# A gated relational graph convolution on one core: the root product moved behind the last relation, three sweeps of edge sums in place of five

## Chip, cores and metric

One core of one Trainium2 chip. The metric is device time of one execution in microseconds (us), median over runs; lower is better. Engines: PE (TensorE), DVE (VectorE), ACT (ScalarE), POOL (GpSimd) and SP (SyncE, which only issues DMAs here).

## What is computed

x is 1250 x 1024, there are 20000 edges (src, dst, type 0 to 7), sorted by dst, and ten 1024 x 1024 matrices: eight relation weights, root, and w_gate (2048 x 1024, two more).

```python
h = maximum(layernorm(x), 0)
u = h @ root + bias
for r in range(8):
    mask = (edge_type == r)
    sums = segment_sum(h[src] * mask[:, None], dst, 1250)
    cnt  = segment_sum(mask, dst, 1250)
    u = u + (sums / maximum(cnt, 1)[:, None]) @ weight[r]
z = concatenate([u, h], 1) @ w_gate + b_gate
out = x + tanh(u) * z + h * (1 - z)
```

## The kernel before

All matrices go through PE as pairs of float16 numbers (a high and a low part), three matmuls for each product of a 128-row block. The relation is applied before the sum: y = h @ weight[r] is written to DRAM (`y_rows`), and the edges then gather rows of y.

**The order of the work** is a list of 325 units, written out by tables of unit numbers. A unit is one piece of a product: all engines walk the same loop `for n in range(NU)`, and each does there what the tables put at n. `GEMMS` is the order of the ten products, `FIRST` the unit at which each starts. The first three (`PLAIN = 3`) and the last are plain products, 20 units of 24 matmuls each. The seven between are Winograd block products (quarters of the matrices, seven phases), 35 units of 12 matmuls each. Before the change:

- plain: rel0 in units 0 to 19, rel1 20 to 39, root 40 to 59
- block products: rel2 from 60, rel3 from 95, rel4 from 130, rel5 from 165, rel6 from 200, rel7 from 235, gate_h (the half of w_gate that meets h) from 270
- plain: gate_u (the half that meets u) in units 305 to 324

PE writes unit n into PSUM bank n % 4 and waits until unit n - 4 has been taken out (`FREED`). In block products DVE does the adding (`finish`, L1069), and for the relations ACT and DVE split the result in high and low part (L766, L1024). Weights are landed, measured (`peek`, L683), split (ACT L716, DVE L937) and, for block products, added in quarters (DVE L953) beside the products.

**The sums.** Edges are cut into 80 groups: ten tiles of 125 destinations by eight relations. A sweep is a set of relations that are summed for all ten destination tiles in turn; `SWEEPS` lists them, and a sweep can start only when its last relation is in DRAM. In a start phase DVE turns dst and type into a key and a row number for each edge (`edge_keys`, L884 to L908; the loop over sweeps at L897 to L906 shifts both for each later sweep), and POOL scatters the edges into a table. Each group is padded to tiles of 128 edges. For each tile POOL copies an index (L623), gathers rows of y (L633) into a ring of five buffers `G`, and makes a one-hot matrix (L641, at the end of a sweep L669). PE multiplies: four matmuls of 512 columns (L1278) into banks 4 and 5 and one for the count (L1281). `AGG_AT[g]` is the unit after which PE does the first tile of group g, `REST_AT[g]` that of its other tiles. DVE then divides and adds to u in `add_group` (L1145 to L1147), at unit `REST_AT[g]`. The first tile of the next group waits for this, since the banks are the same.

**u** (1250 x 1024, float32) lies in DRAM, `u_rows`. A step is one destination tile in one sweep: SP loads the tile to one of three buffers `ub` (`load_u`, L412), the sweep's groups are added, SP stores it (`store_u`, L421). In sweep 0 the load fetches what the root product wrote. After the last sweep u is closed tile by tile: DVE `row_scale` (L1154 to L1159), ACT `u_high` (L774), DVE `u_low` (L1163), ACT `tanh_u` (L780, in place, then stored), PE `turn_u` (16 transposes in two halves, L1313, both into bank 7), ACT and DVE `u_out` (L787, L1172) into hT, from where gate_u reads. `SPLIT_U` and `TURN_U` give the units of these; they are at least three units apart per tile, and `TURN_U` of the last tile is unit 306, inside gate_u. There is one buffer `uhl` for the split u.

**SP's queue** is in order too: at each n it does its landings, then u's stores and loads, then waits for the unit's result (`store`, L398 for y, L402 for the z rows and, before, root's). A wait in it holds back all that follows.

## Time and profile before

| | us |
|---|---|
| median of 3 runs | 1406.08 |
| lowest, highest | 1405.66, 1414.51 |
| span of the profiled execution | 1407.7 |
| PE busy in it | 1291.5 (92%) |
| DVE, POOL, ACT busy | 952.5, 754.8, 409.0 |
| mean granted clock of PE | 0.974 of full speed |
| moved by DMA | 269.44 MB |

The span runs from the first to the last instruction of one profiled execution, and is 1.6 us over the median of the unprofiled runs. Busy time of PE holds matmuls at the lower clock too; DMA issues and waits are not busy time.

### The profile page before, as it was taken

The numbers are of one execution on the slowest core, as the hardware profiler recorded it, in microseconds if no ns is written. First come the engines' busy times: TensorE is split into PE (matmuls) and PEld (weight loads), VectorE is DVE, ScalarE is ACT, GpSimd is POOL, SyncE is SP. The second block draws the span as 40 slices with busy tenths as digits, with TensorE's granted clock in tenths as the row PEclk, the third lists the DMA queues.
The fourth block names the chain that finished last, engine by engine and source line by source line (L and its number), as shares of the span: only waits on it lengthen the run. The fifth ranks groups of instructions, "written<-read, shape, count | busy, mean of one in ns | idle before, by whom it ended". The sixth has DMA issues, their size and how long they took to land.

```text
span 1407.7 us, 20144 instructions
## 1 busy us (share of the span) xinstructions
PE 1291.5 (92%) x6205; PEld 651.6 (46%) x6205; DVE 952.5 (68%) x1260; ACT 409.0 (29%) x501; POOL 754.8 (54%) x837
## 2 busy tenths in 40 slices
PE   2978899999999999999998999998999989786898
PEld 1434344444444445555554445454445445343565
DVE  6889678366565667775675577646666778765777
ACT  5344123214132422321332043223222323432000
POOL 2423088786878426686687558664756464320000
PEclk9998899999999999999999999999999999998999
DMA  6442125215224348777875887769889977648872
GB/s 220 154 173 101 44 52 156 69 45 171 54 59 122 114 158 277 238 237 247 277 209 161 292 267 246 238 210 305 279 254 303 312 230 240 204 138 248 239 226 90
DMA packets 112355, 269.44 MB, mean 191 GB/s; under 512 B 22558, under 2 KB 23061, under 8 KB 112268
## 3 DMA queue, kind: packets, MB, share of 16 engines
q1 hardware_dynamic: 78284, 185.88, 40.2%
q0 software_dynamic: 33984, 82.40, 20.4%
q8 instruction: 55, 0.90, 0.3%
q14 instruction: 32, 0.26, 0.1%
HBM read 203.66 MB, written 87.30 MB: 207 GB/s over the span
## 4 chain that ended last, share of the span: by engine, by line
PE 61%; DVE 13%; DMA 10%; issue 7%; POOL 4%; ACT 2%; DVEq 1%; SPq 1%; POOLq 1%; ACTq 0%
PE ps L1320 52%; PE ps L1278 8%; DMA early<-y_rows,pair 7%; DVE W L937 2%; DMA early<-u_rows 1%; POOL onehot L641 1%; DVE hT L990 1%; DMA W<-in_L_gnn_weight_dram 1%; POOL early L633 1%; DVE hT L985 1%; PE ps L1313 1%; POOL pair L623 1%; DVE early L1147 1%; DVE early L1069 1%; DVE early L1163 1%
## 5 line engine op out<-in xcount | busy, mean ns | idle before, releaser
L1320 PE MATMUL ps<-W,hT 128*128 128x512 f16 (+2 forms) x4740 | 1076.0, 385 | 13.0 <-DVE W L937 13.0
L1320 PEld LDWEIGHTS ps<-W,hT 128*128 128x128 f16 (+2 forms) x4740 | 479.9, 104 | 537.8 <-issue 43.4
L633 POOL DMA_INDIRECT early<-y_rows,pair x200 | 242.1, 1211 | 194.5 <-PE ps L1281 152.4
L606 POOL DMA_INDIRECT table_rows<-edges,table_i x160 | 240.5, 1503 | 100.6 <-issue 100.6
L1278 PE MATMUL ps<-early,onehot 128*125 x800 | 205.9, 385 | 26.6 <-POOL onehot L641 13.1
L641 POOL TENSOR_SCALAR onehot<-iota_d,pair 128x125 f16<-128x125 f16 x185 | 159.9, 864 | 64.2 <-DMA early<-y_rows,pair 58.2
L766 ACT ACTIVATE yhl<-early 128x512 f16<-128x512 f32 x120 | 75.3, 628 | 355.3 <-DVE early L1069 194.2
L937 DVE SCALAR_TENSOR_TENSOR W<-W,wsc 128x2048 f16<-128x2048 f32 x62 | 146.5, 2364 | 13.8 <-ACT W L716 13.7
L1278 PEld LDWEIGHTS ps<-early,onehot 128*125 x800 | 106.8, 137 | 100.4 <-issue 46.6
L716 ACT ACTIVATE W<-W,wsc 128x2048 f16<-128x2048 f32 x62 | 122.6, 1990 | 50.9 <-DVE wsc L932 20.3
L683 ACT ACTIVATE peek_out<-W 128x1024 bf16<-128x1024 f32 x80 | 84.2, 1052 | 94.7 <-DMA W<-in_L_gnn_weight_dram 72.7
L1147 DVE SCALAR_TENSOR_TENSOR early<-ps,inv,early 125x1024 f32<-125x1024 f32 x80 | 102.7, 1284 | 2.8
L1024 DVE TENSOR_TENSOR yhl<-early,yhl 128x512 f16<-128x512 f32 x120 | 83.6, 696 | 0.7 <-ACT yhl L766 0.5
L1069 DVE SCALAR_TENSOR_TENSOR early<-ps,Q 128x512 f32<-128x512 f32 x60 | 41.4, 689 | 50.4 <-PE ps L1320 42.5
L581 POOL TENSOR_TENSOR early<-early 128x1024 f16<-128x1024 f32 (+1 forms) x10 | 27.3, 2729 | 88.5 <-ACT early L731 88.5
L1069 DVE SCALAR_TENSOR_TENSOR early<-ps,hT 128x512 f32<-128x512 f32 x60 | 41.3, 688 | 38.5 <-PE ps L1320 30.8
L623 POOL COPY pair<-edges 128x2 int32 x200 | 60.2, 301 | 11.3 <-DMA y_rows<-yhl 10.0
L1036 DVE SCALAR_TENSOR_TENSOR yhl<-ps,yhl 128x512 f16<-128x512 f32 (+1 forms) x40 | 27.1, 685 | 55.0 <-ACT yhl L758 55.0
L1145 DVE TENSOR_SCALAR inv<-ps,wsc 125x1 f32<-125x1 f32 x80 | 17.3, 216 | 67.5 <-PE ps L1281 52.5
L1069 DVE SCALAR_TENSOR_TENSOR Q<-ps,Q 128x512 f32<-128x512 f32 x60 | 41.1, 685 | 30.5 <-PE ps L1320 30.4
L953 DVE TENSOR_TENSOR W<-W 128x2048 f32<-128x2048 f32 x26 | 59.5, 2288 | 0.1
L758 ACT ACTIVATE yhl<-ps 128x512 f16<-128x512 f32 (+1 forms) x40 | 23.6, 595 | 123.2 <-PE ps L1320 123.2
(184 smaller groups left out, 756.0 us busy)
## 6 DMA issues: line engine op xcount, KB each, us to landing
y_rows<-yhl SPq DMA_DIRECT2D x144, 256.0 KB
W<-in_L_gnn_weight_dram SPq DMA_DIRECT2D x31, 1024.0 KB, 7.4
early<-u_rows SPq DMA_DIRECT2D x52, 448.0 KB
u_rows<-early SPq DMA_DIRECT2D x50, 448.0 KB
W<-in_L_gnn_w_gate_dram SPq DMA_DIRECT2D x8, 1024.0 KB, 8.3
early<-in_x_dram SPq DMA_DIRECT2D x9, 512.0 KB, 4.5
hs_rows<-early SPq DMA_DIRECT2D x9, 512.0 KB, 3.2
u_rows<-yhl SPq DMA_DIRECT2D x18, 256.0 KB
```

Of the source, the lines that this page charges most:

```text
L606: pool.indirect_dma_start(out=table_rows, out_offset=bass.IndirectOffsetOnAxis(ap=at_i[:, c:c + 1], axis=0), in_=packed[0:EP, c:c + 1], in ...
L633: pool.indirect_dma_start(out=G[:, b, :], out_offset=None, in_=y_rows[i], in_offset=bass.IndirectOffsetOnAxis(ap=idx[:, b, :], axis=0), bo ...
L641: pool.tensor_scalar(onehot[:, b, 0:DT], iota_d[:, :], dcol[:, b, :], None, ALU.is_equal).then_inc(s["tile_ready"], 1)
L683: nc.scalar.activation(peek_out[:, :], homes[LAND[w][q]][:, half * D:(half + 1) * D], ACT.Abs, accum_out=wsum[:, w, 2 * q + half:2 * q + h ...
L716: nc.scalar.activation(Wv[MAT[w][c]][:, 0, :], homes[at], ACT.Copy, scale=wscale(w, 0)).then_inc(s["w_hi"], 1)
L766: nc.scalar.activation(yhl[:, o % 4, 0, :], C[:, o % 2, :], ACT.Copy).then_inc(s["y_hi"], 1)
L937: nc.vector.scalar_tensor_tensor(out=Wv[MAT[w][c]][:, 1, :], in0=homes[at], scalar=wscale(w, 0), in1=Wv[MAT[w][c]][:, 0, :], op0=ALU.mult, ...
L1024: nc.vector.tensor_tensor(yhl[:, o % 4, 1, :], C[:, o % 2, :], yhl[:, o % 4, 0, :], ALU.subtract).then_inc(s[YDONE], 1)
L1069: return nc.vector.scalar_tensor_tensor(out=to, in0=part, scalar=scale, in1=of, op0=ALU.mult, op1=ALU.add)
L1147: nc.vector.scalar_tensor_tensor(out=ub[0:DT, b, :], in0=ps[0:DT, 4:6, :].rearrange("p b n -> p (b n)"), scalar=inv[0:DT, 1:2], in1=ub[0:D ...
L1278: nc.tensor.matmul(ps[0:DT, 4 + half, :], hot_t, rows[:, bass.ds(ring_slot * (2 * D) + (half * D + part * HC), HC)], start=first and part ...
L1320: last = nc.tensor.matmul(ps[0:rows, n % 4, :], hT[:, m, v_h, k, n0:n0 + rows], Wh[MAT[w][c]][:, v_w, k, :], start=(first and v_h + v_w == ...
```

## The change

1. `GEMMS` becomes rel0 to rel7, root, gate_h, gate_u. rel2 is now the third plain product (units 40 to 59), rel3 to rel7 start at 60, 95, 130, 165 and 200, and root is a block product in units 235 to 269. Its result goes to an array of its own, `root_rows`, with the additions of a block product (`close`).
2. `SWEEPS` are relations 0 to 2, 3 to 5 and 6 to 7: 30, 30 and 20 groups, at units 100 to 161, 168 to 231 and 238 to 274. Before there were 30, 20, 10, 10 and 10 groups from units 109, 175, 222, 246 and 273 to 300.
3. Sweep 0 starts u from nothing: relation 0 is written by a `tensor_scalar`, and nothing is loaded.
4. u is closed during gate_h, a tile every 2.3 units from unit 280. For each tile SP loads u and root's rows, POOL adds them (a new loop behind its last sweep), then the steps are as before. The split u has two buffers and the transposes banks 4 and 5, one for each half. root's rows and the split u lie in slots of the ring `G`.
5. b_gate gets a row of its own; the inputs of output tile 3 are loaded at unit 305 and no longer at 303, and tiles 3 and 4 swap buffers.

```diff
-    SWEEPS = [(0, 3), (3, 5), (5, 6), (6, 7), (7, 8)]
+    SWEEPS = [(0, 3), (3, 6), (6, 8)]
...
-    GEMMS = ["rel0", "rel1", "root"] + [f"rel{r}" for r in range(2, R)] + ["gate_h", "gate_u"]
+    GEMMS = [f"rel{r}" for r in range(R)] + ["root", "gate_h", "gate_u"]
...
-    AGG_AT = ([109 + g * 66 // 30 for g in range(30)] + [175 + g * 46 // 20 for g in range(20)]
...
+    AGG_AT = ([100 + g * 64 // 30 for g in range(30)] + [168 + g * 66 // 30 for g in range(30)]
+              + [238 + g * 38 // 20 for g in range(20)])
...
+    FINAL = NS * NJ
+    SCALE_U = {FIRST[W_GH] + 10 + 23 * j // 10: j for j in range(NJ)}
+    SPLIT_U = {n + 1: SCALE_U[n] for n in SCALE_U}
+    TURN_U = {n + 3: SCALE_U[n] for n in SCALE_U}
+    TANH_U = {n + 2: SCALE_U[n] for n in SCALE_U}
...
+            def load_root(j):
+                sp.wait_ge(s["u_rooted"], j - 1) if j >= 2 else sp.wait_ge(s["u_added"], NG)
+                for n0, p0, rows in halves(*DTL[j]):
+                    sp.dma_start(root_in[j % 2][p0:p0 + rows, :], root_rows[n0:n0 + rows, :]).then_inc(s[f"root_loaded{j % 2}"], 16)
...
                         if FINAL - 1 <= k < len(STEPS) - 3:
                             load_u(k + 3)
+                        if FINAL <= k < len(STEPS) - 2:
+                            load_root(k - FINAL + 2)
...
+            for j in range(NJ):
+                u = ub[0:DT, (FINAL + j) % 3, :]
+                pool.wait_ge(s[f"u_loaded{(FINAL + j) % 3}"], 32 * u_loads(FINAL + j))
+                pool.wait_ge(s[f"root_loaded{j % 2}"], 32 * (j // 2 + 1))
+                pool.tensor_tensor(u, u, root_in[j % 2][0:DT, :], ALU.add).then_inc(s["u_rooted"], 1)
...
+                if r == 0:
+                    nc.vector.tensor_scalar(ub[0:DT, b, :], sums, inv[0:DT, 1:2], None, ALU.mult).then_inc(s["u_added"], 1)
...
             def row_scale(j):
                 u = ub[0:DT, (FINAL + j) % 3, :]
-                dve.wait_ge(s["u_added"], SPAN[NS - 1][0] + (j + 1) * (SWEEPS[NS - 1][1] - SWEEPS[NS - 1][0]))
+                dve.wait_ge(s["u_rooted"], j + 1)
...
             def turn_u(j, half):
...
+                pe.wait_ge(s["u_lo"], j + 1)
+                if j == 0:
+                    pe.wait_ge(s["u_added"], NG)
                 else:
-                    pe.wait_ge(s["uT_a_out"], j + 1)
-                    turned_b[0] += 1
-                pe.wait_ge(s["wscale_ready"], maxes[0])
-                o = ps[:, 7, :].bitcast(F16)
+                    pe.wait_ge(s["uT_b_out" if half else "uT_a_out"], j)
+                o = ps[:, 4 + half, :].bitcast(F16)
```

Two places where the order of instructions moves. The first is DVE's, in `edge_keys` in the start phase: from the first shift for a later sweep to the packing of row and column. Q holds keys and row numbers in float32, edges the key. Before:

```order
L902 TENSOR_SCALAR Q<-Q 125x160 [waits dve_step]
L897 SCALAR_TENSOR_TENSOR Q<-Q 125x160 [waits dve_step]
L897 SCALAR_TENSOR_TENSOR edges<-Q,edges 125x160 [waits dve_step]
L906 TENSOR_TENSOR Q<-Q 125x160 [waits dve_step]
L897 SCALAR_TENSOR_TENSOR edges<-Q,edges 125x160 [waits dve_step]
L902 TENSOR_SCALAR Q<-Q 125x160 [waits dve_step]
L897 SCALAR_TENSOR_TENSOR Q<-Q 125x160 [waits dve_step]
L897 SCALAR_TENSOR_TENSOR edges<-Q,edges 125x160 [waits dve_step]
L902 TENSOR_SCALAR Q<-Q 125x160 [waits dve_step]
L897 SCALAR_TENSOR_TENSOR Q<-Q 125x160 [waits dve_step]
L897 SCALAR_TENSOR_TENSOR edges<-Q,edges 125x160 [waits dve_step]
L908 SCALAR_TENSOR_TENSOR edges<-Q 125x160 [waits dve_step]
```

(these twelve stand behind five more for the first of the four later sweeps). Now, all of them:

```order
L913 TENSOR_SCALAR Q<-Q 125x160 [waits dve_step]
L908 SCALAR_TENSOR_TENSOR Q<-Q 125x160 [waits dve_step]
L908 SCALAR_TENSOR_TENSOR edges<-Q,edges 125x160 [waits dve_step]
L913 TENSOR_SCALAR Q<-Q 125x160 [waits dve_step]
L908 SCALAR_TENSOR_TENSOR Q<-Q 125x160 [waits dve_step]
L908 SCALAR_TENSOR_TENSOR edges<-Q,edges 125x160 [waits dve_step]
L917 TENSOR_TENSOR Q<-Q 125x160 [waits dve_step]
L908 SCALAR_TENSOR_TENSOR edges<-Q,edges 125x160 [waits dve_step]
L919 SCALAR_TENSOR_TENSOR edges<-Q 125x160 [waits dve_step]
```

Sixteen instructions for later sweeps have become eight; the rest of the start phase stands as it was.

The second place is SP's queue in gate_h, one tile of u in the middle: from the store of its tanh to the next z rows (`early` is where `ub` and the ring lie, `yhl` the buffer of results). Before:

```order
L421 DMA u_rows<-early 112x1024 [waits tanh_ready]
L421 DMA u_rows<-early 13x1024
L412 DMA early<-u_rows 112x1024 [waits u_stored1,u_stored2]
L412 DMA early<-u_rows 13x1024
L402 DMA zh_rows<-yhl 128x512 [waits y_done]
```

Now:

```order
L425 DMA u_rows<-early 112x1024 [waits tanh_ready]
L425 DMA u_rows<-early 13x1024
L411 DMA early<-u_rows 112x1024 [waits u_stored1,u_stored2]
L411 DMA early<-u_rows 13x1024
L416 DMA early<-root_rows 112x1024 [waits u_rooted]
L416 DMA early<-root_rows 13x1024
L403 DMA zh_rows<-yhl 98x512 [waits y_done]
```

The load of root's rows of the tile after next is new, and stands behind the load of u, which itself waits until the store has landed.

## Rows read from the trace of the kernel before

**Rows 1.** The page: busy times; the group of the sums' matmuls (busy us, mean ns | idle before).

```profile
PE 1291.5 (92%) x6205; PEld 651.6 (46%) x6205; DVE 952.5 (68%) x1260; ACT 409.0 (29%) x501; POOL 754.8 (54%) x837
...
L1278 PE MATMUL ps<-early,onehot 128*125 x800 | 205.9, 385 | 26.6 <-POOL onehot L641 13.1
```

**Rows 2.** Busy time by stretch: PE, PEld, DVE, ACT, POOL; then clock, DMA share, GB/s.

```profile
0.00:181.00 181.00, 130.44 (x655) 63.66 (x656) 137.95 (x183) 70.60 (x92) 52.10 (x61) 0.92 0.39 136
...
522.00:744.00 222.00, 219.73 (x1071) 112.76 (x1071) 152.48 (x216) 66.23 (x88) 158.03 (x201) 1.00 0.79 252
744.00:940.00 196.00, 186.10 (x895) 95.01 (x896) 120.53 (x167) 48.71 (x60) 134.60 (x180) 1.00 0.74 232
940.00:1122.00 182.00, 173.67 (x820) 86.62 (x819) 118.61 (x175) 58.42 (x77) 107.35 (x151) 0.98 0.90 293
1122.00:1290.00 168.00, 138.77 (x720) 71.69 (x718) 123.53 (x189) 57.38 (x55) 59.15 (x79) 0.92 0.67 210
1290.00:1403.00 113.00, 104.78 (x491) 66.21 (x489) 79.44 (x92) 2.13 (x3) 0.00 (x0) 0.97 0.67 194
```

**Rows 3.** PE's waits, 1130 to 1290 us: total us, times, longest.

```profile
PE ps L1313 <- DVE early L1163: 20.1, 7, 7.6
PE ps L1278 <- POOL onehot L641: 5.0, 2, 4.0
```

**Rows 4.** PE's waits, 940 to 1037 us.

```profile
PE ps L1278 <- DVE early L1147: 5.7, 4, 2.9
```

**Rows 5.** Timeline of PE after a short idle time: start, us, instruction [idle before].

```profile
948.94 2.75 PE L1320 MATMUL ps<-W,hT 128*128 128x512 f16 x12
954.60 1.07 PE L1278 MATMUL ps<-early,onehot 128*125 x4 [2.92 <-DVE early L1147]
...
955.54 4.44 PE L1320 MATMUL ps<-W,hT 128*128 128x512 f16 x12
```

**Rows 6.** Timeline of the start phase: DVE's keys, and PE.

```profile
53.29 0.24 DVE L902 TENSOR_SCALAR Q<-Q 125x160 f32<-125x160 f32 x1
...
58.72 0.32 DVE L908 SCALAR_TENSOR_TENSOR edges<-Q 125x160 int32<-125x160 f32 x1
...
82.45 1.01 PE L1247 MATMUL ps<-ident_h,early 128*128 128x128 f16 x8 [4.82 <-ACT hT L737]
```

**Rows 7.** Timeline of POOL and PE where the last sweep starts.

```profile
1130.64 0.18 POOL L623 COPY pair<-edges 128x2 int32 x1 [8.29 <-DMA y_rows<-yhl]
...
1138.78 1.19 POOL L641 TENSOR_SCALAR onehot<-iota_d,pair 128x125 f16<-128x125 f16 x1 [1.50 <-DMA early<-y_rows,pair]
...
1140.28 1.96 PE L1278 MATMUL ps<-early,onehot 128*125 x4 [4.04 <-POOL onehot L641]
```

**Rows 8.** SP's waits, 1130 to 1290 us.

```profile
SPq L412 <- DMA u_rows<-early: 37.5, 8, 8.0
```

**Rows 9.** Durations and waits of single kinds of work: DMA to landing; POOL's subtraction of 128 x 1024.

```profile
early<-in_x_dram SPq DMA_DIRECT2D x9, 512.0 KB, 4.5
...
L581 POOL TENSOR_TENSOR early<-early x10: 2120/2126/4144, 9.3 to 129.6; 128x1024 f16<-128x1024 f32 x9, 98x1024 f16<-98x1024 f32 x1
```

**Rows 10.** Closing one tile of u: DVE's timeline; durations by line, ns min/median/max.

```profile
1228.81 1.22 DVE L1154 TENSOR_REDUCE urow<-early 125x1 f32<-125x1024 f32 x1
...
1230.81 0.17 DVE L1159 TENSOR_SCALAR usc<-uexp 125x2 int32<-125x2 int32 x1
...
L774 ACT ACTIVATE early<-early,usc x10: 1132/1150/1152, 1155.2 to 1288.9; 125x1024 f16<-125x1024 f32 x10
...
L780 ACT ACTIVATE early<-early x10: 1038/1057/1057, 1157.7 to 1307.3; 125x1024 f32<-125x1024 f32 x10
...
L1163 DVE SCALAR_TENSOR_TENSOR early<-early,usc x10: 1275/1278/1285, 1156.4 to 1306.0; 125x1024 f16<-125x1024 f32 x10
```

**Rows 11.** Timeline of two of DVE's scans in the start phase.

```profile
69.97 6.83 DVE L990 TENSOR_TENSOR_SCAN hT<-hT 125x3200 bf16<-125x3200 bf16 x1
...
92.82 8.64 DVE L990 TENSOR_TENSOR_SCAN hT<-hT 125x3200 bf16<-125x3200 bf16 x1
```

More of the change, by code:

```diff
@@ L207, in gated_rgcn_preln @@
             SCALE_AT[w] = FIRST[w - 1] + 26
-    SCALE_AT[W_GU] = next(n for n in range(FIRST[W_GH] + 26, FIRST[W_GU]) if n + 1 not in TURN_U and n + 2 not in TURN_U)
     SOURCE = [0, 1, 0, 2, 0, 3, 1]
@@ L300, in gated_rgcn_preln @@
         brow = early[:, 9 * D:10 * D]
+        brow_gate = early[:, 0:D]
+        uhl = [G[:, b, :] for b in (1, 2)]
+        root_in = [G[:, b, :].bitcast(F32) for b in (0, 3)]
         qflat = Q[:, :, :].rearrange("p i n -> p (i n)")
@@ L479, in _ @@
                 if n == 10:
-                    load_brow(bias)
-                if n == FIRST[W_ROOT + 1] + 2:
-                    sp.wait_ge(s[YDONE], 2 * NJ * (W_ROOT + 1))
-                    load_brow(b_gate)
-                if n == AGG_AT[0] - 2:
-                    for b in range(4):
-                        sp.wait_ge(s[f"y_stored{b}"], 16 * NJ * 2 * (W_ROOT + 1) // 4)
-                    for k in range(2):
-                        load_u(k)
+                    load_brow(brow, bias)
+                if n == unit(W_ROOT, 2, 0):
+                    sp.wait_ge(s[YDONE], 2 * NJ * W_ROOT + 1)
+                    load_brow(brow_gate, b_gate)
                 if n == FIRST[W_GU]:
@@ L517, in _ @@
                     load_part(1, "t")
-                    sp.wait_ge(s["u_added"], NG)
-                    for part in ("h", "x", "t"):
-                        load_part(3, part)
             def store_out(j, ready, c):
@@ L1045, in finish @@
                 o = out_no(n)
-                if w == W_ROOT:
-                    half = out_place(o)[2]
-                    rows = LT[out_place(o)[1]][1]
-                    dve.wait_ge(s["gemm_done"], n + 1)
-                    dve.wait_ge(s["brow_loaded"], 16)
-                    dve.wait_ge(s[f"y_stored{o % 4}"], 16 * (o // 4))
-                    nc.vector.scalar_tensor_tensor(out=yf[0:rows, o % 4, :], in0=part[0:rows], scalar=wscale(w, 1)[0:rows],
-                                                   in1=brow[0:rows, half * HC:(half + 1) * HC], op0=ALU.mult,
-                                                   op1=ALU.add).then_inc(s[YDONE], 1)
-                    return
                 if w < PLAIN:
@@ L1229, in _ @@
                     low_weights(w, c)
-                if n - 1 in U_DONE:
-                    row_scale(U_DONE[n - 1])
+                if n in SCALE_U:
+                    row_scale(SCALE_U[n])
                 if n in SPLIT_U:
@@ L1236, in _ @@
         def _(pe):
-            maxes, turned_a, turned_b, seen = [0], [0], [0], set()
+            seen = set()
             def turn_h(i):
@@ L1312, in turn_u @@
                         kk = half * KH + k
-                        last = nc.tensor.transpose(o[:, at:at + DT], uhl[0:DT, v * D + kk * P:v * D + (kk + 1) * P],
+                        last = nc.tensor.transpose(o[:, at:at + DT], uhl[j % 2][0:DT, v * D + kk * P:v * D + (kk + 1) * P],
                                                    ident_h[0:DT, 0:DT])
```

99 lines of the change are left out of this document (46 added, 53 removed).

## Prediction

> **What bounds the kernel now.** I read the busy times first: PE 92%, all others at 68% or less [rows 1]. So the question is not how much the others do, but where PE stands still or runs at its lower clock. The busy times by stretch answer it [rows 2]. In the start phase (0 to 181 us) PE is idle for 51 us. From 522 to 1122 us, where sums and block products alternate, it is idle for only 2.3, 9.9 and 8.3 us in three stretches. From 1122 us (gate_h, the last sweep, u's closing, gate_u) to 1403 us it is idle for 29.2 + 8.2 = 37.4 us, and its mean granted clock is 0.92 and 0.97, which costs 0.08 x 168 + 0.03 x 113 = 17 us if it worked all the time; some of that fell into idle time, so I take 15. That stage loses some 52 us. PE's waits say to whom: 20.1 us, 7 times, for `u_low` (L1163) before a transpose, and 5.0 us for one-hot matrices [rows 3]. [...]
>
> **PE's work does not change.** Root goes from plain (480 matmuls) to block product (420), but rel2 goes the other way. Counting the edges by destination tile and relation, the groups need 188 tiles; rounded up to fives in each sweep that is 75 + 50 + 25 + 25 + 25 = 200 before and 75 + 75 + 50 = 200 now. 800 matmuls, four a tile, agree [rows 1]. The transposes stay 160. So everything has to come out of waits and clock.
>
> **Term 1, the start phase: -3 us.** `edge_keys` loses eight DVE instructions; from 53.29 to 58.72 us fifteen of them take 0.36 us each [rows 6], so 2.9 us. They stand in a stretch in which DVE has hardly a pause, the layer norm of the next rows stands behind them, and PE waits for what comes of it (4.82 us at 82.45) [rows 6]. I take -3. The ends are 0 (another wait comes last) and -6 (the clock also falls less often).
>
> **Term 2, sums and sweeps, units 100 to 275: -2 us.** Two things go against each other.
>
> A sweep that starts three units behind its last relation has to wait. The one in the trace (unit 273) shows the chain: y lands and POOL may go on at 1130.64, the first one-hot begins at 1138.78, PE begins at 1140.28 after 4.04 us idle [rows 7], with the second wait 5.0 us in all [rows 3] and 1.7 us of clock: 7 us. Now two sweeps start so, at 168 and 238. Ahead of the first, PE has four product units (10.4 us) from the last y's matmuls to the first sum, against 9.6 us from landing to PE's start plus some 4 to 5 us for splitting and storing y: 4 us of waiting, 6.5 with clock and the second wait. At 238 DVE's splitting of the last y stands behind root's first unit and the subtraction in its bias row, some 3 us more: 9.5. Together 16 where there were 7: +9.
>
> The sums themselves are closed by DVE one unit before PE wants the banks again. Where DVE is late, PE waits: 5.7 us in four waits in 940 to 1037 us [rows 4], one of them the 2.92 us of [rows 5]. Some of these were DVE waiting for a u tile that had just been stored; u is loaded for adding in 20 steps instead of 50, and has two or three groups' time to come, so these go. On the other hand the last sweep has a group every 1.9 units where the three last ones had one every 2.4 to 3. All idle time in 522 to 1122 us is 20.5 us [rows 2], with clock 24. I take 13 now, -11. The sum of both is -2. The ends: -10, if the first one-hots come in time, and +15, if each of the 19 close handovers in root's product costs a further 0.8 us.
>
> Sweep 0 starts nine units earlier, which only shifts it: its y is in DRAM by unit 60, and in the trace POOL waits there for DVE's turn at the table, not for the table's load.
>
> **Term 3, closing u and gate_u: -10 us.** Of the 52 us, 7 were the sweep's start (term 2), so 45 are to be had. The closing no longer waits for sums, and none of it reaches into gate_u. What is late next is a cycle through DRAM. Root's rows of tile j+2 are loaded only after tile j's tanh has been stored, since SP's queue holds the load of u ahead of it, which waits for that store. From one `row_scale` to that of the tile after next:
>
> - `row_scale` 2.2 us, `u_high` 1.15, `u_low` 1.3, tanh 1.05 [rows 10], and one taking-out of a product unit between them on DVE, 0.75: 6.4 us
> - store: SP stood for 37.5 / 8 = 4.7 us at the next load [rows 8], behind 0.75 us of issuing: 5.4
> - load: 4.5 for 512 KB [rows 9], root's 0.8 later behind u's: 5.3
> - POOL's addition, new: nearest is its subtraction of the same size, 2.1 [rows 9]
> - eight hand-overs of 0.1 each: 0.8
>
> That is 20 us, and 21 in the phases where DVE takes out a unit with two or three instructions. PE needs for two tiles 4.6 units of 2.6 us and 32 transposes in 1.8 us: 13.8. So the cycle is slower than PE by 7.2 us for each pair. Tiles 0 and 1 are loaded in time; from tile 1 to tile 9 there are four pairs, 29 us late at the end. u's copies out of PSUM and the splitting of gate_u's weights stand in the same DVE queue and add some 6 us. 35 us are lost where 45 were: -10. PE's clock adds nothing of its own, since it only fills waits. Ends: with a store of 3.9 and a load of 3.7 (a fifth to a quarter under the rows) the cycle is 18, 25 us are lost, -20; with the longest store wait, 8.0 us [rows 8], and POOL's longest, 4.1 [rows 9], the cycle is 26, which is 12 us over PE's pace, 48 + 6 us are lost, +9; the splitting of gate_u's four weight quarters, which shares DVE's and ACT's queues with the last tiles, may then add 8: +17. I take -10, by the medians.
>
> The loads moved to unit 305 (tile 3, 1.5 MB) are wanted six units of 5.2 us later, behind 3 MB of others; at the 194 GB/s of that stretch [rows 2] 4.5 MB take 23 us of 31. They cost nothing; without that cover it would be up to 6 us.
>
> **Sum.** -3 - 2 - 10 = -15 us. The profiled span of 1407.7 becomes 1392.7; the median is 1.6 us under the span, so 1406.1 becomes 1391.
>
> **A rule against it.** The subtraction on POOL takes 2.1 us at the median and 4.1 at most [rows 9], and a scan of DVE takes 6.83 us alone and 8.64 where one of the long subtractions lies beside it [rows 11]: the two engines hold each other up. The Trainium skill, "SBUF — State Buffer", section "Who interferes with whom", says that a DVE instruction with two inputs from SBUF contends with a GpSimd instruction that reads SBUF, and that the one that comes later blocks fully. By that rule, the rows agree. In gate_h the new addition meets `u_low` and the weights' low halves, both with two such inputs.
>
> **Rivals.**
>
> - Ports: each addition on the cycle takes 4.1 us instead of 2.1. Four pairs make 8 us: 1399. For it: three of ten subtractions were so long. Against it: DVE is idle or waits while POOL adds, since it waits for just that.
> - Dense sums: term 2 ends at +15 while the others hold: 1408, no change. For it: POOL is busy 134.6 us with 180 instructions, three a tile, in 744 to 940 us [rows 2], so 2.2 us a tile with waits on DMA still to come, and in root's product PE takes a tile every 2.9 us. Against it: PE's waits for one-hots are short.
> - Slower: the DRAM cycle of term 3 at its slow end (+17), which begins to cost more than before when a cycle is over 23 us; with term 1 at -3 and term 2 at +1 that is 1421. For it: a store of 8 us was seen, with DMA shares of 0.67. Against it: the gathers are over by then, and the mean is 4.7.
> - Fast: store and load at their quick ends (-20), the closings and starts at theirs (-10), term 1 at -6: 1370.
>
> **How the numbers follow.** The forecast 0.43, ports 0.1, dense sums 0.2, slower 0.13, fast 0.14. The forecast's own range is 1380 to 1402. A difference of under 1% (14 us) is about what a measurement of this kernel cannot tell from none. Over 14 us faster: half of the forecast's cases and a little more, all of the fast ones, a few of the others: 0.47. Slower by that: most of the slow case, 0.11. Between: 0.42. The range 1371 to 1413 leaves out the far part of the slow and fast cases.
>
> **What would show it.** Right: SP waits for u's store about eight times 5 us; DVE stands at `row_scale` for POOL, and PE at a transpose; the closings follow each other every 10 to 11 us; gate_u runs without a wait; two starts of sweeps with idle times of 4 to 8 us; the first unit ends some 3 us earlier behind 60 us. Wrong: closings every 7 us (the cycle is shorter than I take it), PE waiting for DVE's division at most groups of the last sweep, or for z rows at unit 309.

## The result and the profile after

The changed kernel takes 1420.06 us at the median (1412.12 to 1423.08 over nine runs); the kernel before took 1406.77 us beside it. The ratio is 1.0085, with a 95% interval of 1.0063 to 1.0107: slower by 13 us where I forecast faster by 15, and 7 us outside my range.

The page of the profiled execution, busy times and the two groups that answer to [rows 1]:

```profile
span 1420.5 us, 20065 instructions
PE 1294.9 (91%) x6205; PEld 652.5 (46%) x6205; DVE 954.8 (67%) x1247; ACT 404.9 (29%) x496; POOL 776.8 (55%) x833
...
L1281 PE MATMUL ps<-early,onehot 128*125 x800 | 209.4, 388 | 40.8 <-POOL onehot L647 31.0
L647 POOL TENSOR_SCALAR onehot<-iota_d,pair 128x125 f16<-128x125 f16 x191 | 163.7, 857 | 56.7 <-DMA early<-y_rows,pair 50.1
```

PE is busy for 3.4 us longer than before in a span that is 12.8 us longer: 800 matmuls of sums and 4740 of products, as before. Most of the difference is idle time, and the first group says where part of it went. Before, PE's sums waited 13.1 us in all for one-hot matrices; now 31.0 us.

The busy times by stretch (columns: PE, weight loads, DVE, ACT, POOL, each with its count, then granted clock, DMA share, GB/s), cut at the changed kernel's own stages; they answer to [rows 2]:

```profile
0.00:181.00 181.00, 132.25 (x666) 64.69 (x667) 135.18 (x173) 70.72 (x92) 52.92 (x55) 0.93 0.39 137
500.00:740.00 240.00, 231.77 (x1125) 119.02 (x1124) 157.12 (x229) 68.40 (x87) 167.73 (x217) 1.00 0.70 219
740.00:1000.00 260.00, 248.49 (x1194) 126.04 (x1192) 171.21 (x237) 75.06 (x96) 175.00 (x226) 0.98 0.73 231
1000.00:1190.00 190.00, 171.25 (x800) 86.77 (x801) 117.67 (x154) 28.26 (x27) 110.98 (x156) 0.96 0.69 218
1190.00:1320.00 130.00, 100.53 (x531) 49.95 (x529) 94.13 (x142) 54.07 (x54) 25.62 (x10) 0.87 0.70 217
1320.00:1421.00 101.00, 96.17 (x446) 60.61 (x444) 77.69 (x89) 0.00 (x0) 0.00 (x0) 1.00 0.77 219
```

The third and fourth rows hold the starts of the second and third sweep, the fifth the closing of u during gate_h: 29.5 us idle and a granted clock of 0.87. gate_u (the last) runs at full clock with no wait for u.

To set the kernels side by side I walked PE's timelines unit by unit and took from each stretch what its matmuls take at full clock. What is left is lost time (waits and the lower clock), in us:

| units | stage | before | after | forecast of the difference |
|---|---|---|---|---|
| 0 to 60 | start phase | 76.5 | 74.1 | -3 |
| 60 to 100 | products alone | 4.4 | 4.4 | 0 |
| 100 to 275 | sums and sweeps | 41.6 | 58.6 | -2 |
| 275 to 325 | closing u, gate_u | 46.3 | 44.5 | -10 |
| | sum | 168.8 | 181.6 | -15 |

The sum differs by 12.8 us, as the spans do. Of the 17 us that the third row got worse, 168 to 175 and 238 to 244 (now starts of sweeps) went from 5.1 to 20.8; unit 273's start, 7 us before, is gone. The rest of the row did not move one way: 100 to 168 rose from some 3 us to 13 and 244 to 273 from 5 to 13, but 175 to 238, where the kernel before ran its second sweep and most of its third, fell from 18 to 6. The row also holds more work than before: some 176 of the 200 tiles of edges then, all 200 now.

PE's waits in the sums, first of the kernel before (500 to 1130 us, 70 of the 80 groups, up to unit 273's start; total, times, longest):

```profile
PE ps L1278 <- DVE early L1147: 10.4, 9, 2.9
PE ps L1278 <- POOL onehot L641: 8.0, 9, 2.2
```

and after (500 to 1190 us, all sums but the very first, for which PE had waited 2.3 us at 497.68):

```profile
PE ps L1281 <- POOL onehot L647: 28.7, 14, 7.7
PE ps L1281 <- POOL onehot L675: 3.0, 3, 1.6
PE ps L1281 <- DVE early L1155: 2.9, 3, 1.4
PE ps L1281 <- DVE early L1153: 1.4, 1, 1.4
```

Waits for DVE's division fell from 10.4 to 4.3 us, as forecast. Waits for POOL's one-hot matrices rose by 20.7 us. The longest two, 7.7 and 6.5, stand at the starts of sweeps. Here is the first in the timeline of SP, POOL and PE:

```profile
745.51 0.89 SPq L425 DMA_DIRECT2D u_rows<-early  x2
746.49 1.52 SPq L411 DMA_DIRECT2D early<-u_rows  x2
748.05 0.37 SPq L399 DMA_DIRECT2D y_rows<-yhl  x1
...
752.92 0.18 POOL L629 COPY pair<-edges 128x2 int32 x1 [17.47 <-DMA y_rows<-yhl]
...
760.07 0.61 POOL L647 TENSOR_SCALAR onehot<-iota_d,pair 128x125 f16<-128x125 f16 x1 [0.74 <-DMA early<-y_rows,pair]
...
760.99 1.96 PE L1281 MATMUL ps<-early,onehot 128*125 x4 [7.72 <-POOL onehot L647]
```

The issue of the last y ends at 748.42, behind a store and a load of a whole tile of u (1 MB). POOL goes on at 752.92, 4.5 us later, and PE at 760.99. In the start of the kernel before [rows 7], SP had issued y in this order:

```profile
1125.74 2.51 SPq L398 DMA_DIRECT2D y_rows<-yhl  x2
1128.29 0.82 SPq L421 DMA_DIRECT2D u_rows<-early  x2
```

There y went ahead of u, and POOL went on at 1130.64, 2.4 us after its issue ended.

The third longest wait, 4.3 us, is no start. It stands in the middle of the last sweep, and the gather for that tile landed late, in a stretch in which the DMA engines were busy all the time (last line, columns as above):

```profile
1125.43 0.61 POOL L647 TENSOR_SCALAR onehot<-iota_d,pair 128x125 f16<-128x125 f16 x1 [6.02 <-DMA early<-y_rows,pair]
...
1131.05 1.95 PE L1281 MATMUL ps<-early,onehot 128*125 x4 [4.30 <-POOL onehot L647]
...
1118.00:1126.00 8.00, 7.20 (x36) 3.58 (x35) 3.96 (x5) 2.30 (x4) 1.81 (x4) 1.00 1.02 348
```

In the closing (1190 to 1320 us), PE's waits, which answer to [rows 3]:

```profile
PE ps L1312 <- DVE early L1170: 20.8, 5, 7.3
PE ps L1312 <- DVE hT L1179: 8.6, 2, 4.9
```

L1170 is `u_low`, L1179 DVE's copy of the transposes. The time from tile 1's `row_scale` (L1161, at 1208.27) to tile 9's (1295.79) is 87.5 us for eight tiles, 10.9 each; PE alone would need 6.9. This span, "eight steps" below, is my measure of the closing.

### The profile page after: what moved, and what is told of

The parts are those of the page before. It is cut to its first block, busy times and chain, and to the rows that moved or that the text cites. A ratio compares the mean times of both kernels' runs of the same rounds, so it can differ in the third digit from the quotient of the medians.

```text
span 1420.5 us, 20065 instructions
## 1 busy us (share of the span) xinstructions
PE 1294.9 (91%) x6205; PEld 652.5 (46%) x6205; DVE 954.8 (67%) x1247; ACT 404.9 (29%) x496; POOL 776.8 (55%) x833
## 4 chain that ended last, share of the span: by engine, by line
PE 63%; DVE 11%; DMA 9%; issue 8%; POOL 4%; ACT 3%; SPq 1%; POOLq 1%; DVEq 0%; ACTq 0%
PE ps L1319 52%; PE ps L1281 10%; DMA early<-y_rows,pair 6%; POOL onehot L647 1%; DVE hT L1001 1%; DVE W L948 1%; DMA early<-root_rows 1%; DVE hT L996 1%; POOL early L639 1%; DMA u_rows<-early 1%; DVE early L1170 1%; DVE early L1070 1%; DMA y_rows<-yhl 1%; ACT peek_out L695 1%; ACT W L728 1%
## 5 line engine op out<-in xcount | busy, mean ns | idle before, releaser
L612 POOL DMA_INDIRECT table_rows<-edges,table_i x160 | 237.1, 1482 | 99.5 <-issue 60.8
L1281 PE MATMUL ps<-early,onehot 128*125 x800 | 209.4, 388 | 40.8 <-POOL onehot L647 31.0
L647 POOL TENSOR_SCALAR onehot<-iota_d,pair 128x125 f16<-128x125 f16 x191 | 163.7, 857 | 56.7 <-DMA early<-y_rows,pair 50.1
L948 DVE SCALAR_TENSOR_TENSOR W<-W,wsc 128x2048 f16<-128x2048 f32 x62 | 145.8, 2353 | 22.7 <-ACT W L728 22.7
L728 ACT ACTIVATE W<-W,wsc 128x2048 f16<-128x2048 f32 x62 | 122.7, 1992 | 129.2 <-DVE W L964 70.4
L778 ACT ACTIVATE yhl<-early 128x512 f16<-128x512 f32 x100 | 62.7, 627 | 298.9 <-DVE early L1070 172.9
L695 ACT ACTIVATE peek_out<-W 128x1024 bf16<-128x1024 f32 x80 | 84.2, 1053 | 135.2 <-DMA W<-in_L_gnn_weight_dram 70.4
L1047 DVE SCALAR_TENSOR_TENSOR yhl<-ps,yhl 128x512 f16<-128x512 f32 (+1 forms) x60 | 40.8, 686 | 83.4 <-ACT yhl L770 83.3
L1155 DVE SCALAR_TENSOR_TENSOR early<-ps,inv,early 125x1024 f32<-125x1024 f32 x70 | 89.9, 1284 | 2.5
L770 ACT ACTIVATE yhl<-ps 128x512 f16<-128x512 f32 (+1 forms) x60 | 35.5, 596 | 189.8 <-PE ps L1319 189.7
L629 POOL COPY pair<-edges 128x2 int32 x200 | 60.6, 303 | 35.1 <-DMA y_rows<-yhl 35.1
L682 POOL TENSOR_TENSOR early<-early 125x1024 f32<-125x1024 f32 x10 | 25.6, 2567 | 86.7 <-DMA early<-root_rows 86.7
L1035 DVE TENSOR_TENSOR yhl<-early,yhl 128x512 f16<-128x512 f32 x100 | 69.3, 693 | 0.7 <-ACT yhl L778 0.4
L1070 DVE SCALAR_TENSOR_TENSOR early<-ps,Q 128x512 f32<-128x512 f32 x50 | 34.4, 688 | 44.6 <-PE ps L1319 40.8
L1070 DVE SCALAR_TENSOR_TENSOR early<-ps,hT 128x512 f32<-128x512 f32 x50 | 34.4, 689 | 31.5 <-PE ps L1319 25.2
```

What stands on the lines that cost most here:

```text
L612: pool.indirect_dma_start(out=table_rows, out_offset=bass.IndirectOffsetOnAxis(ap=at_i[:, c:c + 1], axis=0), in_=packed[0:EP, c:c + 1], in ...
L647: pool.tensor_scalar(onehot[:, b, 0:DT], iota_d[:, :], dcol[:, b, :], None, ALU.is_equal).then_inc(s["tile_ready"], 1)
L695: nc.scalar.activation(peek_out[:, :], homes[LAND[w][q]][:, half * D:(half + 1) * D], ACT.Abs, accum_out=wsum[:, w, 2 * q + half:2 * q + h ...
L728: nc.scalar.activation(Wv[MAT[w][c]][:, 0, :], homes[at], ACT.Copy, scale=wscale(w, 0)).then_inc(s["w_hi"], 1)
L778: nc.scalar.activation(yhl[:, o % 4, 0, :], C[:, o % 2, :], ACT.Copy).then_inc(s["y_hi"], 1)
L948: nc.vector.scalar_tensor_tensor(out=Wv[MAT[w][c]][:, 1, :], in0=homes[at], scalar=wscale(w, 0), in1=Wv[MAT[w][c]][:, 0, :], op0=ALU.mult, ...
```

## The experiments

Ratios are to the kernel before, with 95% intervals; the changed kernel's is 1.0085 [1.0063, 1.0107]. All edits are to the changed kernel unless said otherwise.

### Root's rows ahead of the store of u

```diff
+                        if FINAL <= k < len(STEPS) - 2:
+                            load_root(k - FINAL + 2)
                         store_u(k)
...
-                        if FINAL <= k < len(STEPS) - 2:
-                            load_root(k - FINAL + 2)
```

> The changed kernel, with SP issuing the load of root's rows of tile j+2 ahead of the store of tile j's tanh and not behind the load of u that waits for that store. Theory (the closing of u runs at the pace of a cycle tanh, store, load of root, POOL's addition, row_scale of the tile after next): the cycle loses 5.4 us or more in each pair of tiles, what is left goes by three tiles and is shorter than PE's pace; row_scale comes every 8 to 9 us and not every 11, PE's waits for transposes between 1190 and 1320 us fall from 29 us to 12 or less, and the time falls by some 20 us, to about 1400. Rival 1 (the cycle of u's own store and load with three buffers sets the pace): row_scale still every 10 us or more, under 5 us gained. Rival 2 (DVE's queue in gate_h, with the weights' low halves, sets it): PE's waits stay over 25 us.

1409.76 us, ratio 1.0017 [0.9991, 1.0042]. The eight steps fell from 87.5 to 75.7 us. So the store of u ahead of root's load was on the cycle, but half of the expected 20 us did not come, by the ratios it is 9.6: something else is nearly as late.

### The last y of a sweep ahead of u

```diff
+                last_y = n + 1 in (FIRST[W_OF[SWEEPS[0][1] + 2] + 1], FIRST[W_ROOT])
+                if last_y:
+                    store(out_no(n))
```

(ahead of u's stores and loads at units 164 and 234, and not again behind them).

> The changed kernel, with the store of the last y of relations 5 and 7 issued ahead of the u store and u load that stand before it in SP's queue (units 164 and 234). Theory (the two sweep starts are long since 1 MB of u is put ahead of the last y, which then lands 4.9 us after its issue instead of 2.4): POOL goes on 4 us earlier at both places, PE's waits of 7.7 and 6.5 us fall to about 4 each, and 7 to 8 us are gained with the clock. Rival (the gather's own latency from POOL's start to the first one-hot, 7 us, and DVE's queue set it): under 2 us gained.

1413.84 us, ratio 1.0074 [1.0045, 1.0102]. The start in the timelines:

```profile
744.97 1.12 SPq L399 DMA_DIRECT2D y_rows<-yhl  x2
...
748.47 1.84 POOL L632 COPY pair<-edges 128x2 int32 x1 [13.18 <-DMA y_rows<-yhl]
...
757.30 1.96 PE L1284 MATMUL ps<-early,onehot 128*125 x4 [4.19 <-POOL onehot L650]
```

POOL goes on 2.4 us after the end of y's issue again, and PE waits 4.2 us in place of 7.7 (at the other start 4.5 and 1.5 in place of 6.5). From the last division of one sweep to the first of the next the starts got 3.0 and 1.9 us shorter. By the ratios the kernel gained 1.5 us, which is inside the interval; its profiled span, 1413.0, is 7.5 us shorter. The traces show the mechanism; what it is worth in time stays open between these two.

### Both

The two edits above in one kernel.

> Both of the two edits above. Theory: the gains lie in different stages and add up: 25 to 30 us under the changed kernel, about 1392, which is 1% under the kernel before. If they hit the same DMA queues, the sum is less than the parts by 5 us or more.

1404.4 us, ratio 1.0005 [0.9978, 1.0031]. By the ratios that is 11 us, the sum of the two alone (9.6 and 1.5), where 25 to 30 were expected. Two orders on SP's queue give back most of what the change lost.

### Root's rows left out

This kernel does not load root's rows for tiles 2 to 9, so u of these lacks h @ root; POOL still adds what lies in the buffers.

```diff
-                        if FINAL <= k < len(STEPS) - 2:
-                            load_root(k - FINAL + 2)
...
-                pool.wait_ge(s[f"root_loaded{j % 2}"], 32 * (j // 2 + 1))
+                pool.wait_ge(s[f"root_loaded{j % 2}"], 32)
```

> The changed kernel, with root's rows loaded for the first two tiles alone; the other eight additions take what lies in the buffers, so root's product is left out of u for them. POOL's ten additions stay, and so does u's own store and load. Theory: the same gain as with the loads issued first (20 us), and 1 to 3 us more for 4 MB less traffic. Rival 1 (u's own store and load set the pace): no gain beyond 3 us. If this gains clearly more than the run with the loads first, root's loads cost by their traffic and not by their place.

1402.06 us, ratio 0.9973 [0.9946, 1.0]; eight steps in 67.6 us. That is 20 us less than in the changed kernel and 8 less than with root's rows first. With root's rows gone altogether the closing still does not reach PE's 55 us. By the ratios the kernel is 6 us faster than with root's rows first, where 1 to 3 were expected, so these loads still cost something where they stand; whether by coming late or by their traffic, this run does not tell.

### Later starts

```diff
-    AGG_AT = ([100 + g * 64 // 30 for g in range(30)] + [168 + g * 66 // 30 for g in range(30)]
-              + [238 + g * 38 // 20 for g in range(20)])
+    AGG_AT = ([100 + g * 64 // 30 for g in range(30)] + [171 + g * 63 // 30 for g in range(30)]
+              + [241 + g * 34 // 20 for g in range(20)])
```

> The changed kernel, with sweeps 1 and 2 begun three units later (171 and 241) and packed more densely behind (63 units for 30 groups, 34 for 20; the last group one unit earlier). Theory (each start waits 10 us in all, 6.5 to 7.7 idle and the rest clock, because the first one-hot comes 15 us behind the last y): three units are 7.8 us, so the two starts cost under 4 us together where they cost 21. Of the 17 us some 5 come back as waits in the dense last sweep: 12 us gained, about 1408. Rival (POOL's pace of 2.7 us a tile bounds the last sweep, so the end of the sums does not move): the last group is closed at the same time, under 3 us gained.

1410.54 us, ratio 1.0016 [0.9987, 1.0044]. PE's waits in 500 to 1180 us:

```profile
PE ps L1281 <- POOL onehot L647: 14.2, 15, 2.3
PE ps L1281 <- issue: 5.2, 8, 1.7
PE ps L1281 <- DVE early L1155: 4.2, 5, 1.9
```

The long waits are gone (2.3 us at most, where 7.7 and 6.5 stood), though the groups are closer to each other. By the ratios 9.7 us came back, net of what the closer groups cost, so the tight starts cost at least that.

### Five and four sweeps with the new order of products

```diff
-    SWEEPS = [(0, 3), (3, 6), (6, 8)]
+    SWEEPS = [(0, 3), (3, 5), (5, 6), (6, 7), (7, 8)]
...
+    AGG_AT = [100 + g * 174 // 79 for g in range(80)]
```

> The changed kernel with the five sweeps of before (relations 0-2, 3-4, 5, 6, 7) under the new order of products; the 80 groups stand evenly from unit 100 to 274, so every sweep begins 16 units or more behind its last relation. u's traffic is 20 loads and 20 stores of 0.5 MB more, edge_keys has its 16 instructions again. Theory (the loss in the sums comes from the two starts that stand three units behind a relation): the starts' 21 us go, 3 us in edge_keys and some 5 us for u's traffic and its waits come back: 12 us gained, 1408. Rival (the density of one group in 2.2 units in all stages costs it): the same waits spread over all groups, no gain.

1417.87 us, ratio 1.0073 [1.0043, 1.0103]: next to no gain (the profiled execution, 1424.32 us, is the slowest of its ten). DVE's waits in 740 to 1190 us name what took the place of the starts:

```profile
DVE inv L1148 <- DMA early<-u_rows: 15.5, 4, 8.2
```

In sweeps of one relation u's tile has hardly left when it is wanted again. The longest of these waits ends at 988.08, and PE stands for 8.2 us until 990.22. The second kernel keeps the even spacing, with the groups at the same units:

```diff
-    SWEEPS = [(0, 3), (3, 6), (6, 8)]
+    SWEEPS = [(0, 3), (3, 5), (5, 7), (7, 8)]
```

> As the run with five sweeps, with four (relations 0-2, 3-4, 5-6, 7): every start is 9 units or more behind its last relation, and u's traffic is 10 loads and 10 stores more than in the changed kernel. Theory: the starts' 21 us go, 1.5 us in edge_keys and 2 us of u's traffic come back: 17 us gained, 1403. Rival (density): no gain. Against five sweeps it tells what a sweep costs by itself: 4 us by the theory.

1401.77 us, ratio 0.9955 [0.9921, 0.999]. Its waits in 500 to 1180 us:

```profile
PE ps L1280 <- POOL onehot L646: 11.9, 11, 3.2
PE ps L1280 <- DVE early L1154: 5.8, 6, 2.1
```

No start waits over 3.2 us, and u is never late. 18 us better than the changed kernel in medians, 20 in spans: about as much as the change lost in units 100 to 275. Since five and four sweeps have their groups at the same units, density is not what separates these two. Four sweeps are between two prices: each start costs PE where it is tight, and each further sweep makes u come back sooner.

### Four sweeps and root's rows first

The kernel with four sweeps, with the first experiment's edit.

> Four sweeps as above and root's rows loaded ahead of the tanh's store. The load alone gained 9.6 us against the changed kernel by the ratios to the kernel before (1.0017 for 1.0085). Theory: both gains add, since one lies before unit 275 and the other behind it: 27 us, 1393, 1% under the kernel before. If the starts had only been hiding a lateness of POOL or DMA, the sum is 10 us less.

1392.02 us, ratio 0.9903 [0.9872, 0.9935]: the two repairs nearly add up (18 and 10 us alone, 26 together, by the ratios), and this beats both kernels.

### Is it the density of groups?

Two kernels: the changed one with sweep 0 spread out, and the one with four sweeps and root first with all groups spread out.

```diff
-    AGG_AT = ([100 + g * 64 // 30 for g in range(30)] + [168 + g * 66 // 30 for g in range(30)]
+    AGG_AT = ([96 + g * 68 // 30 for g in range(30)] + [168 + g * 66 // 30 for g in range(30)]
...
-    AGG_AT = [100 + g * 174 // 79 for g in range(80)]
+    AGG_AT = [92 + g * 182 // 79 for g in range(80)]
```

> The changed kernel with sweep 0's groups a little further apart and earlier (units 96 to 161, one every 2.27 units, in place of 100 to 161, one every 2.13). Question: why units 100 to 168 lost 15.5 us where 5.0 were lost before (groups every 2.2 units then). Theory density: 30 groups at 2.13 units are closer than the sums' chain follows, they take 235 us whatever lies between. Then from the first closing to the last takes 237 to 238 us here, though it spans 65 units in place of 61.9, and the time falls by about 5 us, to 1415. Rival: the loss there has another source (starting u from nothing, what root's old place gave); then the stretch grows by the 3.1 units' products, 8 us, to 243, and the time stays at 1420.

1420.61 us, ratio 1.01 [1.007, 1.0131]. The stretch from the first to the last division grew to 238.7 us, near the 237 to 238 that density says and not 243, but PE now stood 8.0 us before the first group, and no time was won.

> Four sweeps and root's rows first, with the groups evenly from unit 92 to 274, one every 2.30 units, in place of 100 to 274, one every 2.20. Theory density: that kernel still loses a few us to late one-hot matrices and divisions in the sums; 2 to 4 us less, 1389 to 1390. Rival: at 2.2 units PE is no longer held up by the sums, and the first group now waits for the table: 1392 to 1396.

1401.87 us, ratio 0.9962 [0.9939, 0.9984]: worse than its parent by 10 us at the median, by 2 us in the profiled execution. PE stood 15.6 us before its first group. POOL's timeline says why:

```profile
472.49 1.19 POOL L611 DMA_INDIRECT table_rows<-edges,table_i  x1 [2.36 <-issue]
475.76 0.61 POOL L615 DMA_DIRECT2D table_i<-table_rows  x1 [2.08 <-DMA table_rows<-edges,table_i]
...
479.70 0.18 POOL L661 COPY pair<-edges 128x2 int32<-128x2 int32 x1 [2.35 <-DVE edges L1025]
```

The scatter of the edges into the table (L611) goes on until shortly before the table is read back at 475.76 (474.07 in the changed kernel, 481.48 in the kernel before). Unit 100, at some 495 us, is about the earliest at which a sum finds its rows ready.

The density itself is read from the lengths of sweeps with 30 groups. A product unit takes 2.59 us (from one start to the next in PE's timeline):

```profile
152.59 2.75 PE L1319 MATMUL ps<-early,hT 128*128 128x512 f16 x12
155.18 2.75 PE L1319 MATMUL ps<-W,hT 128*128 128x512 f16 x12
```

| kernel, sweep | units from first to last group | us from first to last division | less 2.59 a unit |
|---|---|---|---|
| before, first | 63 | 234.1 | 70.9 |
| four sweeps, first | 63 | 235.7 | 72.5 |
| changed, second | 63 | 235.6 | 72.4 |
| from 96, first | 65 | 238.7 | 70.3 |
| changed, first | 61 | 235.1 | 77.1 |
| later starts, second | 60 | 232.2 | 76.8 |

Sums come to 70 to 72 us where groups are 2.17 units apart or more, and to 77 where they are 2.1 or closer. The sweeps of 30 groups that the table leaves out are wider spread: 70 to 73 us over 63 to 66 units, once 76, and 75 to 77 over 61. So density costs some 5 us a sweep, with a scatter of nearly that size.

At 1.9 units (third sweep of the changed kernel, 50 tiles, 153.8 us over 36 units) 60.6 us are left where two thirds of 72 would be 48. Density alone does not explain that: the last 20 groups leave 60.8 us at 1.7 units (later starts, 143.7 us over 32 units), and at 2.2 units, in the kernels with four sweeps, 59 to 62 (53 in the one with four u buffers, and 52 at 2.3 units). The late gather at 1125 us is one part of it; the rest stays open.

### Eight instructions more in `edge_keys`

They compare and add zero, as many as the change took out.

```diff
+                for i in range(4):
+                    step(nc.vector.tensor_scalar(later_sweep, typ_f, float(i), None, ALU.is_ge))
+                    add(src_f, 0, later_sweep)
```

> The changed kernel with eight more instructions of 0.36 us in edge_keys (four comparisons, four additions of zero times their result), which is what the change took out; they compute nothing new. Theory of term 1: DVE has no pause there, so the first closings come 2.9 us later and the time is 1423. Rivals: another wait comes last and nothing moves (1420); or the clock falls more often and it is 1426.

1420.4 us, ratio 1.0095 [1.0065, 1.0125]. The first division comes 3.2 us later, the last of the first sweep 2.3, the last of the second 0.5, the end 0.8. The 3 us are real where they arise, but the sweeps swallow them: where PE waits for one-hot matrices, a later PE only waits less.

### What sets the pace of the closing?

These three start from four sweeps with root's rows first (1392.02 us, eight steps in 75.9). First a third buffer for root's rows, loaded a tile further ahead:

```diff
-        root_in = [G[:, b, :].bitcast(F32) for b in (0, 3)]
+        root_in = [G[:, b, :].bitcast(F32) for b in (0, 3, 4)]
```

> Four sweeps and root's rows first, with a third buffer for root's rows (the free slot of the ring) and their loads one tile further ahead. In the kernel with root first alone POOL still waited 79.7 us for root's rows in nine additions, and a load of root's rows was issued only 5 to 6 us before its addition. Theory lateness: the load is still the last to come; row_scale from tile 1 to tile 9 falls from 75.9 to 68 to 70 us (67.6 is what is left without root's rows at all), the time by 6, to 1386. Rival traffic: the 5 MB of root's rows slow u's stores and loads wherever they stand in the queue: 75 us and 1392, no change.

1390.47 us, ratio 0.988 [0.9849, 0.9911]; eight steps in 75.9 us, unchanged, where 68 to 70 were expected if root's rows were the last to come. POOL's waits moved from root's rows (83.9 us in nine with two buffers) to u's:

```profile
POOL early L682 <- DMA early<-u_rows: 61.1, 8, 12.6
```

and SP stood 42.5 us in seven waits for u's stores. The next one takes these loads off the cycle: a fourth buffer for u, in the same slot.

```diff
-        ub = early[:, 6 * D:9 * D].rearrange("p (b n) -> p b n", b=3)
+        ub = early[:, 5 * D:9 * D].rearrange("p (b n) -> p b n", b=4)
...
+                        if FINAL <= k < len(STEPS) - 3:
+                            load_u(k + 3)
                         if FINAL <= k < len(STEPS) - 2:
                             load_root(k - FINAL + 2)
                         store_u(k)
```

> Four sweeps and root's rows first, and a fourth buffer for u while it is closed (in the free slot of the ring), so that the load of tile j+3 stands ahead of tile j's store and waits only for that of tile j-1. It tells what the closing's 75.9 us from row_scale of tile 1 to that of tile 9 are made of; a third buffer for root's rows left them as they were. Theory of the DRAM cycle (tanh, store, load, addition, one buffer handed round): with the load off the cycle the eight steps take 62 to 66 us (PE's own pace is 55), the time falls by about 10, to 1382. Rival: traffic and the queue of DVE (uncovering of PSUM, weights, u) set the pace wherever the loads stand: 74 to 76 us and 1391 to 1393.

1384.8 us, ratio 0.9873 [0.9835, 0.9911]; eight steps in 71.6 us, between the two expectations. SP's waits for u's stores fell to

```profile
SPq L416 <- DMA u_rows<-early: 8.2, 2, 7.4
```

and the stretch of those eight steps reads

```profile
1185.00:1257.00 72.00, 59.37 (x348) 28.76 (x347) 63.23 (x108) 38.79 (x43) 21.69 (x8) 0.95 0.75 245
```

DVE is busy for 63.2 of 72 us. The load of u in the DRAM cycle was worth 4 us more; that DVE's queue is what stands behind it is read from its busy share, and not shown. The last moves the addition of root's rows to DVE:

```diff
-                pool.tensor_tensor(u, u, root_in[j % 2][0:DT, :], ALU.add).then_inc(s["u_rooted"], 1)
...
+                nc.vector.tensor_tensor(u, u, root_in[j % 2][0:DT, :], ALU.add).then_inc(s["u_rooted"], 1)
```

> The kernel with four u buffers, with the addition of root's rows on DVE (ahead of row_scale) in place of POOL. Theory ports: POOL's addition takes 2.57 us and DVE's u_low, 1.28 us alone, takes 3.37 us where it begins beside it; without it no u_low and no addition of products takes over 2 us, the step is 1.3 us shorter, and the time falls by 3 to 8 us against the kernel with four u buffers. Rival: DVE gets 10 additions of 1.2 us in a queue that is already the one PE waits for: as much is lost as won, or up to 8 us more.

1385.71 us, ratio 0.9871 [0.9829, 0.9914]; eight steps in 70.4 us. `u_low` now takes 1.28 us each time,

```profile
L1176 DVE SCALAR_TENSOR_TENSOR early<-early,usc 125x1024 f16<-125x1024 f32 x10 | 12.8, 1280 | 4.3 <-ACT early L788 4.3
L1165 DVE TENSOR_TENSOR early<-early 125x1024 f32<-125x1024 f32 x10 | 12.2, 1217 | 0.2 <-DMA early<-root_rows 0.2
```

but DVE carries ten additions of 1.22 us more (67.5 busy of 70.6 us). What it no longer has amounts to the same 12 us: 7.4 us of waits for POOL, 2.1 in `u_low` (1.49 us at the mean before), 2.9 in the subtractions of products (0.98, now 0.69). As much is lost as won. The two last kernels are the fastest of all, 1.3% under the kernel before, and not to be told apart from each other or from the one with three root buffers.

## Why the prediction was wrong

**PE's work, 200 tiles:** right. 800 and 4740 matmuls, as before.

**Term 1, -3 us:** right where it arises (-2.4 in units 0 to 60, +3.2 at the first division with eight instructions more), but worth next to nothing at the end of this kernel, since what PE gains it waits for in the sweeps. I had summed it as if nothing behind it had slack.

**Term 2, -2 us: this is the step that failed; it measured +17.** Two sizes in it were wrong, the second by more than the first: 14 of the 19 us are there.

- "Together 16 where there were 7: +9." The two starts cost 20.8 us, 10.4 each, so +14. I had read the chain from a start in which y left SP ahead of u [rows 7] and had not looked at what stands ahead of y in the new order of SP's queue: a store and a load of u, 1 MB. y's issue came 2.3 us later for it and its landing 4.5 us after that, not 2.4. y first took 3.0 and 1.9 us off the starts; later starts took nearly all, and with them the time fell by some 10. The 1.7 us of clock in this sum is what [rows 5] shows behind one wait of 2.92 us (4.44 us for twelve matmuls that take 2.75). It does not come behind every wait: the changed kernel's waits of 2.3 us before 497.68 and 2.1 us before 568.04 were followed by matmuls at a granted clock of 1.00.
- "All idle time in 522 to 1122 us is 20.5 us, with clock 24. I take 13 now, -11." By the same accounting the sums lost 34.6 us apart from the start before (41.6 - 7) and 37.8 after (58.6 - 20.8): +3. The waits for DVE fell by 6, as argued; those for one-hot matrices outside the starts rose from 8.0 to 16.8, the first group's 2.3 included. The units hold 200 tiles where they held 176, so for each tile they lose about what they did; I had expected that to halve. It did fall to a third in 175 to 238 and rose to either side. I had counted POOL's 2.2 us a tile and used it only in the rival of dense sums. A sweep with groups 2.1 units apart takes some 5 us more than one with 2.2; that POOL's chain of gather and one-hot is what can't follow there is argued from PE's waits, not shown. Density alone does not explain what the last sweep loses, and but for one late gather its cause stays open.

The sentence that sweep 0's earlier start "only shifts it" held only just. The table is done at 474 us and not before; four or eight units earlier still and PE stands 8 or 15.6 us.

**Term 3, -10 us: measured -1.8.** The mechanism was right: gate_u ran without a wait, SP waited seven times for u's store (27.1 us, 3.9 each, where I had 4.7), the closings followed each other every 10.9 us (10 to 11 were forecast), DVE stood at `row_scale` for POOL (22.4 us, six times), and taking root's load off the cycle gave 11.8 of 87.5 us. The size was off by 8: 44.5 us are lost where I had 35. The cycle of two tiles was 21.9 us and not 20 to 21: the eight steps are 32 us over PE's 55 where I had 29. POOL's addition is one part of that, 2.57 us at the mean and 3.46 at most where I took 2.1. Outside the eight steps 12 us are lost where I had 6 for the transposes' copies and the weights in DVE's queue; that with u's own loads out of the way DVE is busy for 88% of the stretch speaks for that queue, but I did not separate this rest.

**The rivals.** Dense sums had term 2 at +15 (chance 0.2) and was nearest to what happened by that number; it gave 1408 only because it left term 3 at -10. Its reason, the close groups of the last sweep, is not where most of the +17 lies: the two starts alone are +14. The slower case gave 1421, nearly the time measured, for another reason: it had term 2 at +1 and term 3 at +17. Its number was right and its mechanism not. Ports is real as a mechanism (below), but moving the addition away from POOL gained nothing.

The two parts of term 2 were also not independent, as the sum had taken them: the same placing of the groups made the starts tight and the sweeps behind them dense.

## What to carry to other kernels

When a change makes one stage start right behind another's last output, list what the DMA queue issues ahead of that output in the new order; a wait that is read from a place with another queue order is not the wait to come. Fewer passes over an accumulator save its traffic but make each start tight and the work between them dense, so price both: here four sweeps beat three and five, by 18 and 16 us at the median, and still by 9 where the three start later. And a cycle through DRAM was shortened first by the order of issues (11.8 us of eight steps here), then by a buffer (4 us); what bounds it then has to be looked for anew, and the engine with the longest queue (DVE, busy 88% of the stretch) is the first to ask.

## What the runs showed of the hardware

A DVE instruction with two inputs from SBUF and a POOL addition did not run side by side: the later one waited for the earlier. From the changed kernel, two moments of the closing in the timelines:

```profile
1234.31 2.34 DVE L948 SCALAR_TENSOR_TENSOR W<-W,wsc 128x2048 f16<-128x2048 f32 x1
1235.70 3.15 POOL L682 TENSOR_TENSOR early<-early 125x1024 f32<-125x1024 f32 x1 [4.76 <-DMA early<-root_rows]
1236.57 3.37 DVE L1170 SCALAR_TENSOR_TENSOR early<-early,usc 125x1024 f16<-125x1024 f32 x1
...
1260.87 1.28 DVE L1170 SCALAR_TENSOR_TENSOR early<-early,usc 125x1024 f16<-125x1024 f32 x1
1260.90 3.46 POOL L682 TENSOR_TENSOR early<-early 125x1024 f32<-125x1024 f32 x1 [6.57 <-DMA early<-root_rows]
```

`u_low` takes 1.28 us alone and the addition 2.35. In the first moment the addition came while DVE split weights (L948, two inputs), took 0.80 us longer for it and ended at 1238.85. `u_low` came 0.87 us behind the addition and had 2.28 us to wait; 2.28 + 1.28 is 3.56, near its 3.37. In the second DVE was 0.03 us ahead, kept its 1.28, and POOL took 3.46, near 2.35 + 1.28. The Trainium skill, "SBUF — State Buffer", section "Who interferes with whom", calls the shared ports an exclusive lock that the later instruction waits for; the trace agrees, in both directions.

With one input the rows differ. The reduction of tile 0's `row_scale` at 1200.64 ran beside an addition and took 1.22 us, as the others did without one. But a `tensor_scalar` of three columns took 2.34 us beside the addition at 1291.66, where its median is 0.17:

```profile
1291.68 2.34 DVE L943 TENSOR_SCALAR wsc<-wexp 128x3 int32<-128x3 int32 x1
```

A store of y was seen by POOL 2.4 us after the end of its issue with no tile of u ahead of it on SP's queue, and 4.5 us after it with a store and a load of u ahead.
